# Attention and ternary feed-forward in one kernel: the order of work in the opening

## What is computed

```python
x = hidden_states                                  # 2 x 2048 rows of 512, f32
x = x + layernorm(attn(layernorm(x)))
x = x + layernorm(ffn(layernorm(x)))

def attn(h):        # 16 heads of 32, 64 latent keys a head
    Q, V = h @ Wq.T + bq, h @ Wv.T + bv
    top, idx = top_k(einsum('bhtd,lhd->bhtl', Q, latent) / sqrt(32), 4)
    weighted = sum of the 4 chosen latent rows, weighted by softmax(top)
    return (weighted + V) @ Wo.T + bo

def ffn(h):         # 512 -> 2048 -> 512
    ternary(W) = clip(round(W / s), -1, 1) * s,  s = mean(|W|) + 1e-8
    return (silu(h @ ternary(W_up).T) * (h @ ternary(W_gate).T)) @ ternary(W_down).T
```

## Time and profile before

| | |
|---|---|
| median of 3 runs | 1028.66 us (1027.9 to 1029.03) |
| the profiled execution | 1029.43 us |
| its span, first to last instruction | 1027.6 us |
| PE busy | 966.2 us (94%) |
| DVE busy | 729.3 us (71%) |
| ACT busy | 513.9 us (50%) |
| POOL busy | 533.6 us (52%) |
| granted TensorE clock, mean | 0.984 |

### The profile page before, as it was taken

One profiled execution on the slowest core, in us unless ns is written; L12 is line 12 of the kernel. 1 busy time (PEld: TensorE's weight loads), 2 busy tenths in 40 slices (PEclk: granted clock), 3 DMA queues, 4 the chain that ended last, 5 costly groups with the idle time before them and its releaser, 6 DMA issues.

```text
span 1027.6 us, 17907 instructions
## 1 busy us (share of the span) xinstructions
PE 966.2 (94%) x5738; PEld 469.4 (46%) x5738; DVE 729.3 (71%) x2666; ACT 513.9 (50%) x801; POOL 533.6 (52%) x451
## 2 busy tenths in 40 slices
PE   3738999999999999999999999999999999999997
PEld 2413544345444544445444454445444454445443
DVE  7898798376893689665993779836895669845433
ACT  5787986445534555345444455345453454433430
POOL 2556266645566446554666546564565545643330
PEclk9868999999999999999999999999999999999999
DMA  9953403532124402233113321243022511212001
GB/s 296 400 108 69 149 1 83 141 73 76 22 42 109 107 11 41 62 92 93 21 34 89 75 69 21 47 116 92 11 41 62 97 37 21 42 41 63 1 1 41
DMA packets 149331, 76.91 MB, mean 75 GB/s; under 512 B 135825, under 2 KB 135825, under 8 KB 148113
## 3 DMA queue, kind: packets, MB, share of 16 engines
q1 hardware_dynamic: 149264, 76.18, 29.5%
HBM read 34.21 MB, written 8.39 MB: 41 GB/s over the span
## 4 chain that ended last, share of the span: by engine, by line
PE 68%; DVE 15%; ACT 5%; POOL 5%; issue 4%; DMA 3%; SPq 0%; DVEq 0%; ACTq 0%; POOLq 0%
PE ug L709 36%; PE ug L728 14%; PE ring L559 10%; PE ring L687 4%; PE ring L605 2%; DVE Lr L1580 2%; DMA X1T<-halves 1%; DMA x_in<-in_x 1%; DVE v L1554 1%; DVE halves L1534 1%; DVE row L1671 1%; POOL halves L1297 1%; DVE sty L1674 1%; DVE stx L1694 1%; DVE ugt L1539 1%
## 5 line engine op out<-in xcount | busy, mean ns | idle before, releaser
L709 PE MATMUL ug<-X1T,TU 128*128 128x512 f16 (+1 forms) x1152 | 245.1, 356 | 6.3 <-DVE ugt L1544 4.2
L1274 POOL TENSOR_TENSOR hT<-ugt,hT 128x512 f16<-128x512 f32 x128 | 166.8, 1303 | 161.1 <-ACT hT L1026 161.1
L709 PE MATMUL ug<-X1T,TG 128*128 128x512 f16 (+1 forms) x1152 | 244.8, 355 | 0.0
L728 PE MATMUL ug<-TD,hT 128*128 128x512 f16 x960 | 210.9, 379 | 0.9 <-ACT TD L905 0.9
L1013 ACT ACTIVATE ugt<-ug,cu 128x512 f32<-128x512 f32 x128 | 87.9, 687 | 203.1 <-PE ug L709 202.2
L709 PEld LDWEIGHTS ug<-X1T,TU 128*128 128x128 f16 x1152 | 110.0, 98 | 116.2 <-DVE ugt L1544 4.9
L709 PEld LDWEIGHTS ug<-X1T,TG 128*128 128x128 f16 x1152 | 112.7, 98 | 108.6
L1539 DVE SCALAR_TENSOR_TENSOR ugt<-ugt,ug 128x512 f32<-128x512 f32 x128 | 87.4, 683 | 99.6 <-ACT ugt L1013 98.3
L728 PEld LDWEIGHTS ug<-TD,hT 128*128 128x128 f16 x960 | 93.2, 98 | 115.8 <-issue 3.0
L1580 DVE MATCH_REPLACE8 Lr<-v,Lb 128x68 f32<-128x68 f32 x512 | 102.3, 218 | 0.0
L1544 DVE SCALAR_TENSOR_TENSOR ugt<-ugt,ug 128x512 f32<-128x512 f32 x128 | 87.9, 687 | 4.4
(11 more groups left out here) (218 smaller groups left out, 1498.5 us busy)
## 6 DMA issues: line engine op xcount, KB each, us to landing
out_dram<-Lr SPq DMA_DIRECT2D x32, 256.0 KB, 3.2
x_in<-in_x SPq DMA_DIRECT2D x7, 1024.0 KB, 5.3
x<-in_x SPq DMA_DIRECT2D x28, 256.0 KB, 3.3
PT<-in_Wd SPq DMA_DIRECT2D x8, 512.0 KB, 6.7
hT<-in_Wu SPq DMA_DIRECT2D x4, 512.0 KB, 8.7
hT<-in_Wg SPq DMA_DIRECT2D x4, 512.0 KB, 15.4
x_in<-in_Wd SPq DMA_DIRECT2D x4, 512.0 KB, 5.1
x_in<-in_x SPq DMA_DIRECT2D x4, 256.0 KB, 4.3
```

Source lines behind the costliest of these rows:

```text
L709: last = pe.matmul(ug[:, 2 * (e % 2) + s, cols], w[:, k, e * P:(e + 1) * P], X1T[:, b, k, cols], start=(k == 0 and b == 0), stop=(k == KD ...
L728: last = pe.matmul(down_bank(kind, t), hT[:, a, e, t * P:(t + 1) * P], td[:, e, :], start=(first and e == of[0] and a == 0), stop=(final a ...
L1274: pool.tensor_tensor(hT[:, 1, e, :], ugt[:, 2 + e % 2, :], hT[:, 0, e, :], ALU.subtract).then_inc(h_lo, 1)
```

## The change

Four places in the hand-written order, across four engines. On ACT the four rows of the next chunk go ahead of V's second copies, and two sums of gate pieces behind them; on POOL the subtractions follow that order, and `ln1_rstd_of(1)` moves ahead of two of V's subtractions. On DVE `ln1_biases(1)` and `weights_lo(2)` go ahead of `tern_total(0)` and `abs_sum(14)`. On PE the gate total moves from the end of the first body to behind the second body's first query block. At the start of the second body `t2_rows(-1, 3)` on ACT goes ahead of `q(1)`, and on DVE `t2_lo(0, 3)` ahead of `round_to(1)`. SP's list does not change.

```diff
--- before.py
+++ after.py
@@ -755,12 +755,13 @@
                     wo(2)
                     pe.wait_ge(tern_step, 1)
                     wo(3)
-                    wait(pe, a32_ready, i, KD, KD)
-                    total(weight_sum(1), tot[:, 1:2], tot_ready, 2, tota_ready)
                     return
                 if att:
                     for m in range(KD):
                         q(m)
+                        if kind == "second" and m == 0:
+                            wait(pe, a32_ready, j, KD, KD)
+                            total(weight_sum(1), tot[:, 1:2], tot_ready, 2, tota_ready)
                 logits_after = (8, 12) if kind == "second" else (6, 10)
                 for half in range(2):
                     upgate(0, half)
@@ -1080,16 +1081,16 @@
                     probs_hi(3)
                     vw_half(2, 0)
                     vw_half(3, 0)
-                    abs_sum(10)
-                    abs_sum(11)
                     s1_rows(1, 0)
                     s1_rows(1, 1)
+                    s1_rows(1, 2)
+                    s1_rows(1, 3)
                     vw_half(0, 1)
                     vw_half(1, 1)
                     vw_half(2, 1)
                     vw_half(3, 1)
-                    s1_rows(1, 2)
-                    s1_rows(1, 3)
+                    abs_sum(10)
+                    abs_sum(11)
                     abs_sum(12)
                     abs_sum(13)
                     t2_rows(0, 0)
@@ -1100,8 +1101,8 @@
                 if kind == "second":
                     q(0)
                     t2_rows(-1, 2)
+                    t2_rows(-1, 3)
                     q(1)
-                    t2_rows(-1, 3)
                     sign(1)
                     sign(9)
                     q(2)
@@ -1318,17 +1319,17 @@
                     shift(3)
                     normalise(2)
                     normalise(3)
-                    for m in range(KD):
-                        low_a_half(m, 0)
+                    low_a_half(0, 0)
+                    low_a_half(1, 0)
                     ln1_rstd_of(1)
-                    s1_lo(1, 0)
-                    s1_lo(1, 1)
+                    low_a_half(2, 0)
+                    low_a_half(3, 0)
+                    for t in range(TT):
+                        s1_lo(1, t)
                     for m in range(KD):
                         low_a_half(m, 1)
                     rstd_y(0)
                     rstd_y(1)
-                    s1_lo(1, 2)
-                    s1_lo(1, 3)
                     rstd_x(0, 0)
                     rstd_y(2)
                     round_to(0)
@@ -1764,10 +1765,10 @@
                     probs_lo(2)
                     ln1_stat(1)
                     probs_lo(3)
+                    ln1_biases(1)
+                    weights_lo(2)
                     tern_total(0)
                     abs_sum(14)
-                    ln1_biases(1)
-                    weights_lo(2)
                     abs_sum(15)
                     y_a(0)
                     y_a(1)
@@ -1788,8 +1789,8 @@
                     y_b(3)
                     t2_lo(0, 2)
                     y_c(0, 3)
+                    t2_lo(0, 3)
                     round_to(1)
-                    t2_lo(0, 3)
                     round_to(9)
                     round_to(4)
                     round_to(12)
```

## The result

The changed kernel takes 1031.27 us (median of 10 runs, 1030.40 to 1031.89), the kernel before beside it 1029.05 us (10 runs, 1027.90 to 1030.48). The ratio is 1.0021, 95% interval 1.0012 to 1.0030: some 2.2 us slower, right at the 0.2% that I had called the edge of what can be told from no change. Forecast: 1030.4, range 1027.9 to 1032.4. The 2.2 us lie just outside the 2.06 us that I had called no change, to which I gave 0.60, and in "slower by more", to which I gave 0.35.

The account below looks back on a forecast made before the run. PE bounds the kernel outside the opening, mostly DVE inside it. At the first tanh 2.1 + 0.3 - 0.7 = +1.7 us: 1029.43 to 1031.1 profiled, which lies 0.77 above the median, so 1030.4; range 1027.9 to 1032.4.

Parts of the forecast that it names:

- DVE, the term that decides: DVE's opening: `nb` 1.2 us earlier, but slower low halves bring Wo's first row +2.1 us; bounds -0.4 and +2.3.
- The turns on the halves: Wo's low halves: two-SBUF-input DVE instructions alternate with POOL's, 1.0 us per 512 columns; 0.5 + 0.6 + 1.1 + 1.1 us.
- The sum: DVE's 1.13 us sum, formerly inside `nb`'s wait, is now paid after Wo's halves; cancels against `nb` 1.2 us earlier.
- I let powers block nobody: POOL's powers beside DVE: assumed to hold up no DVE instruction, from an update taking 0.75 us beside one.
- The bound of 0.4 us faster at Wo's first row: Low end for DVE: no turns lost, power unblocked, DVE done at 78.0, PE's low products startable 0.4 us earlier.
- The rows ahead, costed at nothing: ACT and POOL: V's copies and subtractions end some 2 us later, but Wo's third tile has room.
- The gate total, costed at nothing: PE's 0.35 us total behind the first query block: nothing waits; queries start near 88.8 instead of 91.50, at full clock.
- the third rival: The rows were the bound: if the chain ran through the query blocks, 4.8 us earlier queries give 1025; 5%.
- The second chunk's start: Swaps on ACT and DVE: last X1T gains 1.2 us, landing at 109.1; at the tanh +0.3 and -0.7.
- ACT's work up to the tanh is the same list in another order: Second chunk's start: ACT's 0.91 us wait for a rounding stays, +0.3 taken; its 0.69 before the tanh goes.
- Turns not lost: Wo's low halves: DVE's queued halves keep ahead of POOL, -0.4 at Wo's first row, -0.8 in all, 1027.9; 22%.
- The clock: PE at gate/up: idles of 2.9 and 3.2 us may halve its speed, 1 to 2 us more, 1031.9; 23%.

Follow-up runs that it names:

- e3: Kernel before with only DVE's new order (`nb` and Wo's low halves ahead of the total and first sum), POOL's power unmoved: 1030.09 us, ratio 1.0006.
- e1: The change with DVE's order of before (total and first sum ahead of `nb` and Wo's low halves): 1030.39 us, ratio 1.0013.
- e10: Kernel before with only POOL's power for LayerNorm 1 moved between V's second and third subtraction of each half: 1030.54 us, ratio 1.0016.
- e4: Kernel before with only the next chunk's rows ahead of V's second copies on ACT and POOL, the power behind V's four first subtractions: 1030.78 us, ratio 1.0012.
- e12: The change with the sum ahead of `nb`, LayerNorm 1's power late, and y's power ahead of V's last two second subtractions: 1030.75 us, ratio 1.0015.
- e5: Kernel before with only PE's gate total moved behind the second body's first query block: 1031.49 us, ratio 1.0022.
- e6: Kernel before with only the two swaps at the second chunk's start, on ACT and DVE: 1029.18 us, ratio 1.0003.
- e9: Kernel before with POOL waiting for Wo's four low halves before the next chunk's rows, and PE's first total ahead of the second weighing: 1029.23 us, ratio 1.0001.
- e2: The change with the next chunk's rows and the gate total where they were before; DVE's order, early power and swaps kept: 1030.82 us, ratio 1.0012.
- e8: The change with POOL's power for LayerNorm 1 back behind V's fourth first subtraction: 1031.63 us, ratio 1.0021.
- e7: Kernel before with the low half of chunk 0's third probabilities on POOL instead of DVE: 1030.63 us, ratio 1.0012.

## Why the prediction was right, and where it was not

The sign, the place and the size hold: forecast 1.7 us at the first tanh, measured 1.82 from the common zero; forecast 1030.4, measured 1031.27. That 1.7 and 1.82 lie so close is luck: at Wo's first row the forecast was 0.4 us too high, and from there to the tanh it took off 0.4 where the profile adds 0.1. By its steps:

- **DVE, the term that decides.** Wo's first row was to come 2.1 later and came 1.71 later. `nb` starts at 2.16 (74.23), as forecast (2.2). The halves were to take 2.56 + 3.3 us and took 5.02. The turns on the halves were priced too high, 3.3 for 2.46, and one was put in the wrong place: V's third subtraction, issued at 74.17, took its turn from `nb` (0.62 us instead of 0.16), so that 2.9 us were lost to turns in all. The power ran from 72.16 to 74.20, 1.9 us forecast and 2.04 measured.
- **The sum.** Costed at nothing against the earlier `nb` and called a wash; e3 shows its price where `nb` is not early, 1.12, and e1 what it is worth in the change, 0.87.
- **The early power.** "I let powers block nobody" is a step that failed. The power blocks no DVE instruction, but it stands for 2 us itself, and I followed only `nb` behind it: V's third and fourth subtraction stand behind it too, and PE's high products behind those. The bound of 0.4 us faster at Wo's first row took PE's low products to be earlier; they are later, and e10 gives +1.24. In the change it is hidden by DVE, with a few tenths to spare: the last high products end at 79.7, the low ones start at 80.71, and DVE reads the tile at 82.05 without a wait. So it was luck that this step did no harm.
- **The rows ahead, costed at nothing.** Wo's third tile had its room in the change: its last product starts at 85.65, DVE reads it at 88.24. What I left out is POOL's power for y behind the same list. Alone, the rows cost 1.7 us at the first y update by it (e4). With that mended and the other two delays gone, 1.0 came at the third tile (e12), most of it by the clock.
- **The gate total, costed at nothing.** Right in the change, wrong alone (e5, +2.9): it leans on the rows. The queries started at 88.67 as forecast and ran at full clock; none of it reached the tanh, which also drops the third rival.
- **The second chunk's start.** The last X1T subtraction ran in 0.69 us at 103.90. Half 1 behind its transpose starts at 108.88, forecast 109.1, which is 0.54 later than before where the sign is 2.06 later: the swap gains 1.5 there (forecast 1.2). But this part was to give -0.4 at the tanh and gave +0.1, and the swaps alone +0.17. "ACT's work up to the tanh is the same list in another order" is the other step that failed: the new order makes ACT wait 0.89 us for tile 3's bias (102.39; 0.88 in e6), which I costed at nothing. Nor was the 0.69 us of idle before the tanh wholly the swaps' to win: it goes without them in e9 and e10, whose last X1T transposes land 4.12 and 4.15 us after their issue, where the kernel before shows 4.80. So the tanh of its one profile may be late by up to 0.7 us, and the tanh column too low by as much.
- **The rivals.** Turns not lost: refuted by e2 and e9 beside the change. The clock: both idles came (2.93 us as forecast, then 1.30 instead of 3.2), it fell behind the first, and half 0 warmed PE again, which was the argument against that rival; half 1 is at full clock.

The costs do not add. The single delays at the first y update (1.1 for the sum, 1.2 for the power, 1.7 for the rows on POOL) sum to 4.0; the change shows 1.69. They run beside each other on DVE, PE and POOL and end within some 0.7 us. In the change PE's tile is done some 0.3 us before DVE reads it (where DVE waits, in e1, e5 and e10, it reads 1.06 us behind the start of the low products, which is 9.70 here against 9.98), and POOL's power for y ends 0.64 before the update (85.67 against 86.31). So undoing one of them (e1, e2, e8) gives back between nothing and 0.6 us at the tanh. Open stay two things: what of PE's lateness is the idle's and what is chance of the clock, and the difference between a run's shift in time and its shift at the tanh, -0.5 to +0.8 us over the table. It is within the intervals of the medians, but it is above zero in ten of the thirteen rows, as it would be if the tanh of the kernel before were late in its one profile.

## What to carry to other kernels

Before a reordering is costed, write down for each point where the bounding engine reads something how late every producer may be, not only the last one: here three chains ended within 0.7 us of each other, so a term hidden in one version was the bound in the next. A small instruction moved ahead of others on a shared engine is priced by what it waits for and by everything queued behind it, down to the idle it makes on PE. And test "free" parts alone: the rows and the gate total were free only beside the other parts.

## What the runs showed of the hardware

- **A POOL power does not block DVE, but DVE blocks it.** The kernel before had DVE's update at 84.25 in 0.75 us beside a power; in the change the one at 86.31 took 0.75 too, beside a power from 86.03 to 86.60. A power of 4 columns issued behind DVE's 1024-column subtraction takes 2.04 us (the change, e1, e2, e10), against 1.04 in the kernel before, where DVE stood idle beside it. The Trainium skill ("SBUF — State Buffer", on the two sides of SBUF) has one instruction hold the pair's shared port and the other blocked fully; the blocking of the power agrees, its not blocking DVE does not.
- **A short DVE instruction pays the full turn.** 64 columns, 0.23 us, stood 2.04 us behind POOL's 1024 (e7).
- **The clock's return differs between profiles of the same instructions.** Among Wo's first high products PE went to full speed at 3.9 us from the zero in the kernel before and in e3 and e6, at 6.3 in e5, whose list is the same up to there; that moved Wo's first row by 0.44 us. With 1.31 us of idle instead of 0.29 it was 6.1 at the earliest (e1). A part of a stage's shift of half a microsecond can be this and nothing of the edit.
- **The landing of a transpose differs too.** Behind the same work of DVE and with the same list on SP, the last X1T transpose took 4.80 us from issue to landing in the kernel before, 4.38 in e3, 4.15 in e10 and 4.12 in e9.
